# A linear-attention stage that transposes its tokens on VectorE by way of DRAM instead of on TensorE

## What is computed

```python
x = x + window_attention(group_norm(x))            # 7x7 windows, 4 heads, shifted
t = tokens(x)                                      # [16, 3136, 128]
qkv = ln(t) @ W.T + b
q, k = elu(q) + 1, elu(k) + 1
num = einsum('bti,btij->btj', q, cumsum(k_i v_j, axis=time))
den = einsum('bti,bti->bt', q, cumsum(k, axis=time)) + 1e-6
t = t + num / den                                  # linear attention, causal
t = t + ffn(ln(t))    # y_t = sigmoid(batch_norm(W ln(t)) + y_(t-1) V^T), along time
```

## Time and profile before

| | us |
|---|---|
| median of 3 runs (1781.41 to 1783.42) | 1782.33 |
| the profiled execution | 1784.76 |
| its span, first to last instruction | 1782.8 |
| PE busy | 1749.7 (98%) |
| DVE busy | 1509.8 (85%) |
| ACT busy | 1269.8 (71%) |
| POOL busy | 1073.7 (60%) |
| data moved by DMA | 188.30 MB |

### The profile page before, as it was taken

How to read it: one execution, slowest core, us unless ns; L and a number is a source line. 1 busy time by engine, 2 the same in 40 slices (tenths; PEclk the granted TensorE clock), 3 DMA queues, 4 the chain that set the end, 5 groups by cost and what they waited for, 6 DMA issues and landing times.

```text
span 1782.8 us, 58142 instructions
## 1 busy us (share of the span) xinstructions
PE 1749.7 (98%) x19648; PEld 1587.7 (89%) x19648; DVE 1509.8 (85%) x4546; ACT 1269.8 (71%) x3387; POOL 1073.7 (60%) x1202
## 2 busy tenths in 40 slices
PE   7999999999999999989999999999999999989997
PEld 6888888888888888879999999999999999989997
DVE  7889888888888888778888888888888888868787
ACT  5877778887887788856666666666666666657776
POOL 6887888888888888843333333333333333368874
PEclk9999999999999999999999999999999999999999
DMA  5333343433333332313334434343434443457774
GB/s 167 105 103 104 104 110 99 109 107 102 110 103 104 106 106 70 83 43 70 73 67 68 70 68 70 68 67 68 70 68 70 68 68 70 86 178 277 291 278 176
DMA packets 361816, 188.30 MB, mean 106 GB/s; under 512 B 221760, under 2 KB 348720, under 8 KB 356656
## 3 DMA queue, kind: packets, MB, share of 16 engines
q1 hardware_dynamic: 360368, 183.40, 41.0%
q10 hardware_dynamic: 1152, 1.13, 0.2%
HBM read 106.58 MB, written 77.87 MB: 103 GB/s over the span
## 4 chain that ended last, share of the span: by engine, by line
PE 52%; issue 28%; POOL 17%; DVE 1%; DMA 1%; POOLq 0%; ACT 0%; ACTq 0%; SPq 0%; DVEq 0%
POOL la_rstd L1025 12%; PE k_psum L349 7%; PE k_psum L299 6%; PE k_psum L292 6%; PE k_psum L1488 6%; PE k_psum L317 6%; PE k_psum L333 6%; PE k_psum L365 5%; PE k_psum L1478 5%; PE k_psum L283 5%; POOL la_spread L1019 3%; POOL la_tn L1030 2%; DMA wa_group<-in_group 0%; POOLq L42 0%; DMA t<-la_tn 0%
## 5 line engine op out<-in xcount | busy, mean ns | idle before, releaser
L1019 POOL TENSOR_SCALAR la_spread<-la_mv 128x4 f32<-128x4 f32 (+1 forms) x203 | 46.2, 228 | 476.1 <-DVE la_mv L1130 476.0
L618 POOL TENSOR_TENSOR wa_prob<-wa_prob,wa_peak 128x784 f32<-128x784 f32 x128 | 195.0, 1523 | 116.8 <-DVE wa_peak L484 116.8
L966 ACT ACTIVATE la_ve<-k_psum 128x256 f32<-128x256 f32 x196 | 75.6, 386 | 231.9 <-PE k_psum L847 231.9
L1025 POOL TENSOR_TENSOR la_rstd<-la_spread,k_exponent 128x4 f32<-128x4 f32 (+1 forms) x203 | 207.8, 1024 | 17.2 <-POOL la_spread L1019 0.4
L625 POOL TENSOR_TENSOR wa_prob<-wa_prob,wa_inv 128x784 f32<-128x784 f32 x128 | 195.2, 1525 | 11.3 <-DVE wa_inv L445 11.3
L835 PE MATMUL k_psum<-la_uT,la_wt 128*128 128x256 f32 x784 | 201.9, 380 | 0.0
L1085 DVE SCALAR_TENSOR_TENSOR la_fqk<-k_psum,la_raised 128x512 f32<-128x512 f32 x196 | 135.4, 691 | 72.8 <-ACT la_raised L958 72.6
L1562 ACT ACTIVATE sc_y<-k_psum,sc_cols 128x128 f32<-128x128 f32 x414 | 152.3, 368 | 51.9 <-PE k_psum L1488 8.8
L476 DVE TENSOR_TENSOR wa_prob<-k_psum,wa_bias 128x784 f32<-128x784 f32 x128 | 124.9, 976 | 66.2 <-PE k_psum L317 66.1
L1488 PE MATMUL k_psum<-sc_y,sc_vT 128*128 128x128 f32 x824 | 171.0, 289 | 0.0
L958 ACT ACTIVATE la_raised<-k_psum,la_minus_one 128x512 f32<-128x512 f32 x196 | 134.8, 688 | 43.9 <-PE k_psum L835 43.7
(11 more groups left out here) (137 smaller groups left out, 5205.3 us busy)
## 6 DMA issues: line engine op xcount, KB each, us to landing
la_xc<-x SPq DMA_DIRECT2D x196, 128.0 KB, 3.0
wa_xT<-in_x_cm SPq DMA_DIRECT2D x124, 196.0 KB, 3.3
sc_tb<-t SPq DMA_DIRECT2D x17, 1320.0 KB, 8.3
out<-sc_ob SPq DMA_DIRECT2D x17, 1280.0 KB, 5.4
wa_xw<-in_x_tok SPq DMA_DIRECT2D x64, 224.0 KB, 2.7
wa_xw<-in_x_tok SPq DMA_DIRECT2D x64, 168.0 KB, 2.3
x<-wa_y SPq DMA_DIRECT2D x64, 168.0 KB, 2.8
x<-wa_y SPq DMA_DIRECT2D x48, 224.0 KB, 2.9
```

The costliest lines, as they stand in the source:

```text
L618: nc.gpsimd.tensor_tensor(s, s, peak[:, k % S, :].unsqueeze(2).broadcast_to([128, PAIRS * HEADS, WIN]), ALU.subtract).then_inc(lowered, 1)
L1025: nc.gpsimd.tensor_tensor(rstd[:, n % S, used], spread[:, used], exponent[:, used], ALU.pow).then_inc(rooted, 1)
```

## The change

The tokens reach `uT` in another way. POOL writes `u` as rstd * x + (1 - mean * rstd) (two small instructions make that shift), laid out as 32-wide squares. Once per two units SP stores `u` to a new DRAM tensor `squares` (one DMA of 256 KB), and three steps later loads it back with four DMAs of 64 KB, one for each group of 32 channels, so that each 32x32 square lies on the partitions of its channels, still untransposed inside. DVE's 32x32 block transpose then makes `uT` of one unit in one instruction. PE's two transposes, ACT's copy and DVE's two normalising instructions are gone. POOL's normalising and the statistics run five steps further ahead (`AHEAD` 12 for 7, first step -10 for -4), `xc` has 14 slots for 8, `JOIN` is NU - 9 (SP joins at w = 116, the others at 119, POOL at 120; step 0 stays at the same w on every engine), and `uT` and `raised` have fewer slots.

```diff
-        JOIN = NU - 3
+        JOIN = NU - 9
...
+        XC = 14
+        RS = 2
+        TS = 3
+        US = 2
+        AHEAD = 12
...
+        u = sb("u", [P, US, QUADS, 4, SQ])
+        us = sb("us", [128, US, QUADS, 4, SQ])
+        uT = sb("uT", [128, TS, 2 * P])
+        raised = sb("raised", [128, RS, 4 * P])
...
-        steps = range(-4, UNITS + 9)
+        steps = range(-10, UNITS + 9)
...
+                    at_least(sp, attended, n - XC + 1)
+                    sp.dma_start(xc[:, n % XC], rows(x1, n)).then_inc(loaded[n % XC], 16)
+
+                def store_normed(n):
+                    if not inside(n, UNITS) or n % 2 == 0:
+                        return
+                    m = n // 2
+                    sp.wait_ge(normed, n + 1)
+                    sp.dma_start(squares[m], u[:, m % US].rearrange("p q a r -> p q (a r)")).then_inc(u_stored[m % US], 16)
+
+                def load_squares(n):
+                    if not inside(n, UNITS) or n % 2 == 1:
+                        return
+                    m = n // 2
+                    sp.wait_ge(u_stored[m % US], (m // US + 1) * 16)
+                    at_least(sp, u_out, 2 * (m - US) + 2)
+                    for q in range(QUADS):
+                        sp.dma_start(us[q * SQ:(q + 1) * SQ, m % US].rearrange("p k a r -> p k (a r)"),
+                                     squares[m, :, q, :].rearrange("(k p) r -> p k r", p=SQ)).then_inc(u_loaded[m % US], 16)
...
-                    load(n + 4)
+                    load(n + 10)
+                    load_squares(n + 3)
                     store(n - 5)
+                    store_normed(n + 7)
...
-                    turn_tokens(n + 1)
...
-                    turned_out(n + 1)
...
+                    if inside(n, UNITS):
+                        pool.wait_ge(rooted, n + 1)
+                        nc.gpsimd.tensor_tensor(shift[:, n % S, :], mv[:, n % S, 0, :, 0], rstd[:, n % S, 0:2], ALU.mult).then_inc(lowered, 1)
+                        pool.wait_ge(lowered, n + 1)
+                        nc.gpsimd.tensor_scalar(shift[:, n % S, :], shift[:, n % S, :], -1.0, 1.0, ALU.mult, ALU.add).then_inc(shifted, 1)
...
+                    pool.wait_ge(shifted, n + 1)
+                    at_least(pool, u_stored[n // 2 % US], n // 2 // US * 16)
+                    for a in range(2):
+                        last = nc.gpsimd.tensor_scalar(u[:, n // 2 % US, :, n % 2 * 2 + a, :], quads(xc[:, n % XC, a, :]), rstd[:, n % S, a:a + 1],
+                                                       shift[:, n % S, a:a + 1], ALU.mult, ALU.add)
+                    last.then_inc(normed, 1)
...
-                    statistics(n + 3)
-                    remember(n + 3 - AHEAD)
+                    normalise(n + 7)
+                    statistics(n + 8)
+                    remember(n + 8 - AHEAD)
...
+                    dve.wait_ge(u_loaded[n // 2 % US], (n // 2 // US + 1) * 16 * QUADS)
+                    at_least(dve, qk_ready, n - TS + 1)
+                    at_least(dve, v_ready, n - TS + 1)
+                    nc.vector.transpose(uT[:, n % TS, :], us[:, n // 2 % US, :, n % 2 * 2:n % 2 * 2 + 2].rearrange("p k a r -> p a k r")).then_inc(u_out, 1)
...
-                    measure(n + 3)
+                    measure(n + 8)
...
-                    normalise(n + 2)
-                    aggregate(n + 3)
+                    turn_tokens(n + 2)
+                    aggregate(n + 8)
```

More of the change, by code:

```diff
@@ L85, in build @@
     with ExitStack() as ctx:
-        linear = linear_attention(nc, ctx, x1, t2, attn_wt, attn_b, masks_d, ident, ones, exponent, gram, bank,
+        linear = linear_attention(nc, ctx, x1, squares, t2, attn_wt, attn_b, masks_d, ident, ones, exponent, gram, bank,
                                   ffn, signals, (ffn_w, ffn_wt, ffn_vt, gamma, beta))
@@ L653, in _, with linear_attention @@
                 pipeline(step, **run, following=linear["gpsimd"](pool), join=JOIN + 1, prepare=(23, 24))
-def linear_attention(nc, ctx, x1, t2, attn_wt, attn_b, masks_d, ident, ones, exponent, gram, bank,
+def linear_attention(nc, ctx, x1, squares, t2, attn_wt, attn_b, masks_d, ident, ones, exponent, gram, bank,
                      ffn, signals, ffn_data):
@@ L686, in linear_attention @@
         rstd = sb("rstd", [P, S, 4])
-        u = sb("u", [P, S, 2, C])
-        uT = sb("uT", [128, S, 2 * P])
-        raised = sb("raised", [128, S, 4 * P])
+        shift = sb("shift", [P, S, 2])
+        u = sb("u", [P, US, QUADS, 4, SQ])
+        us = sb("us", [128, US, QUADS, 4, SQ])
+        uT = sb("uT", [128, TS, 2 * P])
+        raised = sb("raised", [128, RS, 4 * P])
+        bias, fold = raised[:, 0, 0:3 * C], raised[:, 1, 0:3 * C]
         fqk = sb("fqk", [128, S, 2, 2 * P])
@@ L702, in linear_attention @@
         folded = sem("la_folded")
-        loaded = [sem(f"la_loaded{i}") for i in range(XS)]
+        loaded = [sem(f"la_loaded{i}") for i in range(XC)]
+        u_stored = [sem(f"la_u_stored{i}") for i in range(US)]
+        u_loaded = [sem(f"la_u_loaded{i}") for i in range(US)]
         stored = [sem(f"la_stored{i}") for i in range(XS)]
@@ L815, in tensor @@
                 yield
-                def turn_tokens(n):
-                    if not inside(n, UNITS):
-                        return
-                    if n == 0:
-                        pe.wait_ge(*released["u"])
-                    pe.wait_ge(normed, n + 1)
-                    at_least(pe, u_out, n)
-                    for a in range(2):
-                        mm = nc.tensor.transpose(b_u[:, a * P:(a + 1) * P], u[:, n % S, a, :], ident[:, :])
-                    mm.then_inc(u_turned, 1)
                 def queries_and_keys(n):
@@ L943, in scalar @@
                 yield
-                def turned_out(n):
-                    if not inside(n, UNITS):
-                        return
-                    act.wait_ge(u_turned, n + 1)
-                    at_least(act, qk_ready, n - S + 1)
-                    at_least(act, v_ready, n - S + 1)
-                    nc.scalar.activation(uT[:, n % S, :], b_u[:, 0:2 * P], ACT.Identity, bias=plus_one[:, 0:1]).then_inc(u_out, 1)
                 def exps(n):
@@ L956, in exps @@
                     act.wait_ge(qk_ready, n + 1)
-                    at_least(act, qk_out, n - S + 1)
-                    nc.scalar.activation(raised[:, n % S, :], b_qk[:, :], ACT.Exp, bias=minus_one[:, 0:1]).then_inc(qk_raised, 1)
+                    at_least(act, qk_out, n - RS + 1)
+                    nc.scalar.activation(raised[:, n % RS, :], b_qk[:, :], ACT.Exp, bias=minus_one[:, 0:1]).then_inc(qk_raised, 1)
                 def values_out(n):
```

51 lines of the change are left out of this document (20 added, 31 removed).

## The result

The changed kernel takes **1861.96 us** (median of 4 runs, 1856.92 to 1866.39), the kernel before 1782.12 (1781.41 to 1783.42): a ratio of 1.0446, 95% interval 1.0419 to 1.0474. It was forecast at 1750, in a range of 1738 to 1778. The profiled execution has a span of 1855.2 us where before had 1782.8.

What follows compares the result with a forecast made beforehand. PE was taken as the bound, without gaps at 3.98 us per unit. -43.1 + 10 = -33 us took the profiled 1784.8 to 1751.7, or 1749.3 against the median of runs, rounded 1750; range 1738 to 1778.

Steps and rivals of the forecast that it cites:

- PE, -43.1 us: Linear attention: two transposes of 0.22 us per unit leave PE, over 196 units, saving 43.1 us.
- the landing L = 3.1 us of the path through DRAM: Loads of squares, issue to arrival: 3.1 us, taken from the median of the xc loads.
- The 0.67: Share of time the DMA engines are busy in linear attention: 0.25 for squares plus 0.42 for old traffic.
- the round: Closed round of SP issuing loads, landing, DVE's work: 3.15 us per unit, hidden under 3.76; binds at L = 4.3.
- The sign that the prediction named for this: Linear attention, if wrong: DVE waits for squares in every second unit, with PE idle behind it.
- the prediction's own formula: Time per unit of the closed round through DRAM: (1.9 + L + 1.3) / 2 us.
- the term of 1.9 us: From DVE having attended to SP's last load of squares issued: 0.38 x 4, gaps, 0.2 of lateness.
- squares come late: Rival: loads of squares queue behind other stores; at L = 5.2 a unit takes 4.2 us, 1835 us in all; chance 0.13.
- SP, 5.7 of 7.5 us: SP's issuing per two units: 3.8 us now plus 1.9 added, so SP is not the bound.
- DVE's transpose, 0.34 us: Block transpose of 256 columns: half of 669 ns for 512 columns, 0.67 at the upper end; no cost.
- POOL, 2.7 us per unit: Linear attention: normalising and shift raise POOL from 1.46 to about 2.7 us, under 3.76; no cost.
- The junction, +10: Where window and linear loops meet: POOL's added work and SP's blocked x1 stores cost 10 us, ends 0 and 17.

Runs made afterwards that it cites:

- e5_pad40: The changed kernel with the t2 pieces widened from 33 to 40 floats (160 bytes, a multiple of 32): 1755.95 us, ratio to before 0.9845.
- e12_pad40_pool: The changed kernel with t2 pieces of 40 floats and the store of squares issued by POOL instead of SP: 1752.30 us, ratio to before 0.9815.

## Why the prediction was wrong, by its own steps

- **PE, -43.1 us: right** as a size, once nothing else binds: -41.0 with 40 floats, -43.4 with POOL's store as well.
- **The step that failed is the landing L = 3.1 us of the path through DRAM, and with it the DMA share.** The 0.67 was added up from bandwidths in other stages: it held until 900 us (0.65). After that, engine time per byte is another. The 132-byte pieces are cut at both ends in blocks 1 to 6, and in the kernel before this cost a share of 0.40 to 0.42 instead of 0.37 and landings of 3.1 instead of 2.2, hidden under a full PE. With the squares beside them the share is 0.85, L is 4.5 for squares (5.6 for xc), above the 4.3 at which the round was to bind. The sign that the prediction named for this came: DVE waited for squares 29 times in the 34 pairs of units from 1000 to 1300 us, with PE's gaps behind it.
- **L alone does not give the size.** By the prediction's own formula 4.5 makes (1.9 + 4.5 + 1.3) / 2 = 3.85 us per unit; from 902 to 1551 us a unit took 4.45. The rest is in the term of 1.9 us, which took for granted that SP is free when DVE has attended. SP's issues became dearer as well: its rows from 1000 to 1300 us add up to 272 us, 8.0 per pair where 5.7 was summed. Whether the landing or SP's issuing ends last was not separated.
- The rival "squares come late" named the mechanism (1835 us with L = 5.2, at 0.13). That its 4.2 us per unit lies close to the average of 4.32 is partly luck, since it stands on L = 5.2 and an SP that is never late. Its reason, queues behind short t stores, pointed at the right transfers, but it is their addresses and not their number: e5_pad40 has as many.
- The trace of before held a hint: the earlier trace rows read for 820 to 900 us as well would have shown L stepping up.
- **SP, 5.7 of 7.5 us: wrong, and near the limit.** Four loads take 1.9 us in the median and not 4 x 0.38, the store 0.5, and four t stores 2.0 even with 40 floats (1.6 to 2.9), where the sum had 1.5 for a group. SP's rows of e5_pad40 from 1000 to 1300 us add up to 271 us for 40 pairs, 6.8 each. It does not bind there, for PE is full; with less room than was thought it became part of the loss once the crowded engines slowed the issues.
- **DVE's transpose, 0.34 us: it takes 0.445**, between the ends of 0.34 and 0.67. No cost. The Trainium skill (VectorE: DVE Perf Modes, "Rules for kernel authors") had spoken against the change; in e12_pad40_pool the loop gained what the PE rows had said (43.4 us), so here the trace was to be followed.
- **POOL, 2.7 us per unit:** a normalising instruction takes 0.45, not 0.37; covered in the steady part as said.
- **The junction, +10: it cost 14.6** (14.8 by the common clock), with the waits that were forecast at the residual. Who waited for whom after, 700 to 850 us:

```profile
DVE wa_y L456 <- DMA x<-wa_y: 17.6, 4, 6.9
```

  Four waits, which end near 747, 764, 780 and 784 us. The size lies within its ends of 0 to 17; the third and fourth wait, 5.6 and 0.8 us, were counted as 1 us. But its split was off: freeing SP's blocked queue gives 2 us, the rest stays, and POOL's rounds of 7.5 to 8.8 us take its place.
- With the junction at 14.6 the prediction's sum gives 1753.8, and e5_pad40 gives 1755.95: the forecast was right for a kernel whose small stores are aligned. Its chance of 0.66 took for granted that the transfers already there cost in every stretch what they cost in the one that was read. (The upper end of the range, 1778, adds up only from the profiled execution of 1784.8; from the median it is 1776. Neither matters here.)

## What to carry to other kernels

When a change loads a resource that was hidden, ask what that resource's price is in each stretch, not its mean, and look in the kernel before for steps that nobody waited for. Give small pieces in DRAM a length and a base that are multiples of 32 bytes, as here: the padding was free in the old kernel and decided the sign of the change. And before building on an issuing queue's price per DMA, add up its rows in a stretch where the DMA engines are busy. To compare two traces at a point, measure from a row that the change leaves alone: starts that were 1.8 us apart here meant 3.3.

## What the runs showed of the hardware

- Moving the destination of 160-byte pieces by 4 bytes raised the main queue's share from 59.3% to 82.3% (820 to 900 us) at less data. The Trainium skill (DMA: Bandwidth & Descriptors, "Specifications") says that transfers below 512 bytes make the engine read, modify and write. By that rule alone pieces of 160 bytes would cost the same in either place; the runs do not agree, since in place they give 1756 us and moved 1901. The Trainium skill (Collectives: The Full Stack, "Rules for kernel authors") asks for 32-byte alignment of the buffers of collectives, so that the hardware need not read, modify and write; the sign agrees, though pieces with one cut end cost little here (1759.82 against 1755.95 us, and 66.9% against 62.7% of the queue).
- The dear writes are paid by the others: in the kernel before, xc lands in 3.1 us beside the two-cut pieces and in 2.2 beside blocks 0 and 7.
- Even aligned, the blocks are not alike. In e5_pad40 xc lands in 3.0 to 3.2 us and the queue's share is 63 to 66% beside blocks 1, 3, 4 and 6 (as from 900 to 990 us); beside blocks 0, 2 and 5 it is 2.4 to 2.5 us and 60 to 61% (as from 991 to 1080). The first four are those whose pieces cross a multiple of 256 bytes in `t2`. No run tests this.
- Issuing slows with the engines: from 1000 to 1300 us the same line issued four t stores in 2.0 us in the median (at most 2.9) at a share of 0.64, and in 3.1 us (at most 5.2) at 0.85.
- The block transpose of 256 columns with strided input took 445 ns, that of 512 columns 669.
